# Asking for the next pair's self mask at the beginning of each iteration, ahead of the rounds of weight parts

## The reference

```
def step(t, p):
    tn = _ln(t, norm_g, norm_b)
    t = _mha(tn, tn, skv, sq, sow, sob, tgt_mask) + t      # self-attention, mask 8 x 112 x 112
    tn = _ln(t, norm_g, norm_b)
    t = _mha(src, tn, ckv, cq, cow, cob, src_mask) + t     # cross-attention over 375 tokens
    tn = _ln(t, pg, pb)
    t = t + (jax.nn.relu(tn @ w1 + b1) @ w2 + b2)
    return (t, None)
out, _ = jax.lax.scan(step, tgt, stacked)
```

## Time and profile before

| | before |
|---|---|
| median of 3 runs | 2954.28 us (2951.63 to 2956.06) |
| time of the profiled execution | 2950.49 us |
| its span (first to last instruction) | 2948.5 us |
| TensorE matmul busy | 2807.1 us (95%) |
| VectorE busy | 1713.6 us (58%) |
| ScalarE busy | 1304.0 us (44%) |
| GpSimd busy | 1129.8 us (38%) |
| mean granted TensorE clock | 0.99 |

### The profile page before, as it was taken

One profiled execution on the slowest core, in us unless ns is written; L12 is line 12 of the kernel. 1 busy time (PEld: TensorE's weight loads), 2 busy tenths in 40 slices (PEclk: granted clock), 3 DMA queues, 4 the chain that ended last, 5 costly groups with the idle time before them and its releaser, 6 DMA issues.

```text
span 2948.5 us, 64849 instructions
## 1 busy us (share of the span) xinstructions
PE 2807.1 (95%) x24616; PEld 2329.9 (79%) x24616; DVE 1713.6 (58%) x6432; ACT 1304.0 (44%) x4273; POOL 1129.8 (38%) x1313
## 2 busy tenths in 40 slices
PE   6878999999999999999999999999999999999999
PEld 4656887887887887887887887888888888888887
DVE  3445664664664664655665665665655655655655
ACT  2224544544544543544544444444444444444444
POOL 2203443443443443444433444433443433333333
PEclk9999999999999999999999999999999999999999
DMA  6205234336334336333335243344352334332330
GB/s 211 93 15 192 85 131 157 85 106 201 85 131 151 90 106 194 86 137 118 109 121 157 104 155 99 117 131 142 118 157 79 129 112 121 117 100 78 110 104 24
DMA packets 178762, 350.32 MB, mean 119 GB/s; under 512 B 17997, under 2 KB 142486, under 8 KB 169110
## 3 DMA queue, kind: packets, MB, share of 16 engines
q1 hardware_dynamic: 168086, 195.18, 22.9%
q0 software_dynamic: 10368, 151.00, 14.1%
HBM read 307.48 MB, written 38.67 MB: 117 GB/s over the span
## 4 chain that ended last, share of the span: by engine, by line
PE 81%; DVE 6%; POOL 5%; DMA 4%; issue 2%; ACT 2%; SPq 0%; DVEq 0%; POOLq 0%; ACTq 0%
PE proj L665 18%; PE sum L986 16%; PE score L665 13%; PE proj L685 7%; PE sum L685 7%; PE sum L665 5%; PE proj L1007 3%; PE score L839 2%; DMA smask<-self_mask 2%; PE sum L863 2%; PE proj L944 2%; PE tr L850 1%; PE tr L944 1%; POOL stage_parts L549 1%; PE proj L657 1%
## 5 line engine op out<-in xcount | busy, mean ns | idle before, releaser
L622 POOL TENSOR_TENSOR prob<-prob,rtotal 128x375 f32<-128x375 f32 x672 | 543.5, 811 | 648.4 <-DVE rtotal L1590 647.4
L1063 ACT ACTIVATE prob<-prob,negmax 128x375 f32<-128x375 f32 (+1 forms) x686 | 418.0, 609 | 439.1 <-DVE negmax L1581 406.7
L986 PE MATMUL sum<-pT,ctx 32*128 32x224 f32 (+1 forms) x4608 | 500.6, 358 | 14.8 <-DVE qcT L1573 14.8
L986 PE MATMUL tr<-pT,ctx 32*128 32x224 f32 (+1 forms) x4608 | 500.6, 358 | 0.0
L986 PEld LDWEIGHTS sum<-pT,ctx 32*128 32x128 f32 (+1 forms) x4608 | 417.9, 185 | 68.1 <-issue 62.6
L1581 DVE CUSTOM_DVE_ANT_0 prob<-score,cbias 128x375 f32<-128x375 f32 x672 | 357.4, 532 | 183.2 <-PE score L665 179.5
L986 PEld LDWEIGHTS tr<-pT,ctx 32*128 32x128 f32 (+1 forms) x4608 | 417.0, 185 | 0.0
L1599 DVE STREAM_TRANSPOSE pT<-prob 128x384 f32<-128x384 f32 x672 | 373.5, 559 | 0.0
L665 PE MATMUL score<-ctx_parts,qc_high 128*128 128x376 f32 x1344 | 368.2, 355 | 0.0
L579 POOL TENSOR_TENSOR prob<-prob,rtotal 112x448 f32<-112x448 f32 x200 | 186.3, 931 | 452.2 <-DVE rtotal L1451 452.2
L1142 ACT ACTIVATE prob<-prob,negmax 112x112 f32<-112x112 f32 x800 | 298.8, 376 | 85.9 <-DVE negmax L1469 85.9
(11 more groups left out here) (240 smaller groups left out, 5249.8 us busy)
## 6 DMA issues: line engine op xcount, KB each, us to landing
w_vq_parts<-sa_v_parts POOLq DMA_DIRECT2D x24, 2048.0 KB, 8.7
w_kf_parts<-sa_k_parts POOLq DMA_DIRECT2D x24, 2048.0 KB, 8.4
w_vq_parts<-sa_q_parts POOLq DMA_DIRECT2D x24, 2048.0 KB, 8.7
w_kf<-ff_w SPq DMA_DIRECT2D x48, 1024.0 KB, 7.0
ctx<-ctx SPq DMA_DIRECT2D x192, 176.0 KB
stage<-sa_kv SPq DMA_DIRECT2D x24, 512.0 KB, 3.8
sa_v_parts<-stage_parts SPq DMA_DIRECT2D x12, 1024.0 KB, 5.5
sa_q_parts<-stage_parts SPq DMA_DIRECT2D x12, 1024.0 KB, 4.8
```

The source lines that it names most:

```text
L622: pool.tensor_tensor(row, row, rtotal[:, G * SG + i:G * SG + i + 1].broadcast_to([P, S2]), ALU.mult).then_inc(prob_ready, 1)
L986: ins = pe.matmul(bank[:, 0:HT * R], ctx4[keys_of, m // (HALVES // NB), j, :], pT[keys_of, m % 2, :, j * R:(j + 1) * R], start=j == 0, sto ...
L1063: act.activation(o, i, ACT.Exp, bias=negmax[0:rows, col:col + 1], scale=scale, accum_out=total[0:rows, col:col + 1]).then_inc(exp_ready, 1)
```

## The change

The wait for `smask_used` and the request for the next pair's self mask move from between the two rounds to the beginning of the iteration's part in `sp`'s program, ahead of the new layer's waits and of the first round. No instruction is added or removed, and no other program is touched.

```diff
@@ -475,6 +475,8 @@
                 next_p = (p + 1) % PAIRS
                 new_layer = p == PAIRS - 1 and l < L - 1
                 rounds = rounds_in(it)
+                sp.wait_ge(smask_used, it + 1)
+                load_pair_smask(next_p)
                 if new_layer:
                     sp.wait_ge(resid_ready, at.at("resid", 1))
                     load_out_bias(0, "sa_ob", l + 1)
@@ -483,8 +485,6 @@
                 for r in rounds[0:1]:
                     store_parts(r)
                     load_raw(r + 1)
-                sp.wait_ge(smask_used, it + 1)
-                load_pair_smask(next_p)
                 if new_layer:
                     sp.wait_ge(resid_ready, at.at("resid", 2))
                     load_out_bias(1, "ca_ob", l + 1)
```

## The result

The changed kernel takes 2911.18 us (median of 4 runs, 2910.12 to 2913.32) against 2955.17 us (4 runs of before, 2951.63 to 2956.94): ratio 0.9854, interval 0.9836 to 0.9871. That is 44.0 us faster; 2915.8 was forecast. Its profiled execution took 2911.07 us with a span of 2909.0, so between the two profiled executions 39.4 us went, where the working said 38.5.

The account below looks back on a forecast made before the run. The prediction took the self mask's late load, delaying VectorE's sum1 copy for TensorE, as the bound. Intervals gave 38.6 us, waits 38.2; 38.5 off the 2954.28 median gave 2915.8 us, range 2908 to 2928.

Parts of the forecast that it names:

- What bounds: Main loop: TensorE waits 26.3 us for VectorE's copy of sum1, VectorE 26.2 us for the self mask's late load.
- Rival (c): Mask request early but landing late, or TensorE waits for something else at the query projection: 2954.28 us, chance 0.05.
- The move is free for SyncE: SyncE's earlier mask request: issue of 0.43 to 1.69 us fits its 21 us gap, so it costs nothing.
- rival (d): Request behind the context's requests holds SyncE and delays the second round: slower, 2971 us at a 10 us slip; chance 0.03.
- What goes, by intervals, 38.5 us: Loop intervals between second copies into v: surplus 39.26 us less iteration 0's 0.70 gives 38.6; 38.5 taken.
- sum by waits, 38.2: TensorE at the sum1 copy: 25.9 us waits, 4.2 for resuming, 8.1 for slow matmuls behind the five longest waits.
- The median, 2915.8: Whole kernel's timed median: 2954.28 us shown, less 38.5, gives 2915.8 us.
- Quick conversion: VectorE's mask conversion ends before GpSimd's cast starts: 0.34 us, no collisions in the 15 iterations, unlike iteration 0's 1.45.
- the margin of 0.53: Iteration 1: the conversion was to end 0.53 us before GpSimd's cast starts, at 1.48 us after the copy's start.
- Rival (a): GpSimd's cast meets VectorE's conversion in each round iteration, stretching it to 1.45 us: 2926.3 us, chance 0.11.
- 15 collisions: Upper bound of conversions meeting GpSimd's cast: all 15 at 0.70 us each, 10.5 us given back.
- Rival (b): Five clock falls in the loop stay or new ones come, keeping 8.1 us: 2923.9 us, chance 0.10.

Follow-up runs that it names:

- the second experiment: Kernel before, mask request moved behind the second round's store; its rival, the mask's wait only a bystander, gave at most 2960 to 2980 us. Measured 3118.51 us, ratio 1.0568.
- the run with nine repeats: Changed kernel with VectorE repeating the mask's conversion nine times, making TensorE wait without a transfer: 3028.69 us, ratio 1.0255.

## Why the prediction was right

- *What bounds:* right. The wait of 26.2 us for the mask was the cause, not a bystander: early masks or a later conversion give the time back, and later masks cost more. Rival (c) and the rival of the second experiment fall with that.
- *The move is free for SyncE:* right. Issue 1.58 us in a gap of 22; rival (d) had no start. GpSimd's first softmax row of iteration 8 keeps 5.67 us of slack where 6.3 were worked out.
- *What goes, by intervals, 38.5 us:* 38.0 measured in the loop. The sum by waits, 38.2, held as well, with its three terms: the waits, 0.28 for resuming, the clock's falls. Two later intervals, 110.35 and 110.27 us, are no more 110.0 than iteration 0's; they were as long before, hidden under their waits.
- *The median, 2915.8:* 4.6 us too high. The step that failed is the base: the gain of the profiled execution was taken off a median that stood 3.8 us above it, as if these 3.8 us would stay. They did not: the changed kernel's medians are 2911.18 and 2911.66, near the 2912.0 worked out for the profiled execution, beside medians of before of 2955.17 and 2950.88. The Trainium skill ("TensorE: Matmul & The Clock Gate", "What's actually happening") has the clock watched without regard to the kernel's start; by it the text put the median near 2912 and did not count it. The runs fit this as far as they go: waits of the same 2.1 us had a fall in two of thirteen places, and the spread of before, 4 to 10 us over seven runs, is 2 or 3 over the changed kernel's four. That the 3.8 us were falls in just these waits stays open. The part ahead of the loop moved by up to 6 us between profiled executions, and could account for them as well.
- *Quick conversion:* right, 0.34 us in all iterations but the first. The raw half did land earlier without its neighbour: in iteration 1 the cast starts 1.25 us after the copy into v instead of 1.48, which leaves 0.30 us of the margin of 0.53, the smallest of any iteration in this execution. That no cast met a conversion was close.
- *Rival (a)* was the one with teeth: 20 us where every iteration meets a cast. Its price in the prediction, 0.70 per collision, was near what a cast alone costs (0.59 with the smaller cast) and too low for two in a row (1.55). Its 15 collisions count iteration 0, which has one already; 14 could come.
- *Rival (b):* refuted. No stretch of 10 us in the loop is below full clock any more.

## What to carry to other kernels

A small load that nobody thinks of can stop the main engine through the program order of another: look in the waits for a pair of rows with like totals, and ask what stands behind the waiting instruction. Then request it at the first place where its buffer is free; how much earlier than needed made no difference here. Reckon a gain from the profiled execution against that execution, and if what goes includes the waits behind which the clock falls, don't count on the difference to the timed median to stay.

## What was not expected of the hardware

- A fall of the granted clock cost, besides the wait and 0.28 us, 1.5 to 1.6 us behind waits of TensorE of 2.1 to 3.0 us (1.6 and 1.9 in the run with nine repeats), 1.6 to 3.3 behind waits of 3.7 to 5.3 us, and 1.5 to 3.1 behind waits of 10 to 12 us. So a wait four times as long doesn't bring a dearer fall. Length alone doesn't decide whether one comes either: a wait of 1.66 us had one, three of 1.67 to 1.71 us in the kernel before had none, and of thirteen of 2.1 us two had one. From 2.14 us on all had one.
- The Trainium skill ("SBUF — State Buffer", section "SBUF: two separate sides") gives the port pair that GpSimd shares with VectorE's two-port modes to whichever instruction starts first. Here a conversion by VectorE that had started 0.27 us ahead took 0.34 to 0.37 us alone or beside a plain GpSimd copy of 128x375, 1.35 us beside a cast of 128x896, and 2.32 us through two casts. That is not what the page gives for the one that starts first, and the measurement decides. The two GpSimd instructions differ in size as well as in kind, and which of the two makes the difference was not tried.
- A mask of 98 KB took 3.3 us from issue to landing at best in the changed kernel and 5.3 at the median, where most stand right behind the context's requests. It took about 10 us where GpSimd's 2 MB load had been asked for 0.5 us before; whether that load or the new layer's weights ahead of it in SyncE's queue holds it up is open.
